# Second layer of a four-layer recurrent kernel: logits beside B and C, state product on column groups, next tile's first steps inside the last expert

## The reference

```python
# mixer: Mamba-2 (SSD), 8 heads of 64, state 16
zxbcdt = u @ W_in.T                       # z 512, x 512, B 16, C 16, dt 8
dt  = softplus(zxbcdt[..., -8:] + dt_bias)
xBC = silu(causal_conv4(xBC))
y   = ssd(x * dt, A * dt, B, C) + x * D   # chunked scan
y   = rmsnorm(y * silu(z)) * norm_w
s   = y @ W_out.T
# ffn: 8 experts, all computed, gated by a 1.5-entmax found by 25 bisection steps
logits = xt @ Wr + br
gates  = entmax_bisect(logits, n_iter=25)
h = relu(xt @ W1[e] + b1[e]);  y = h @ W2[e] + b2[e];  out = sum_e y * gates[:, e]
```

## Time and profile before

| | |
|---|---|
| median of 3 runs | 4324.44 us (4317.86 to 4325.86) |
| the profiled execution, its own time | 4321.67 us |
| its span in the trace | 4319.8 us |
| mean granted TensorE clock | 0.987 |
| PE busy | 4179.0 us, 97% |
| DVE busy | 2288.0 us, 53% |
| ACT busy | 1636.5 us, 38% |
| layer 1 in the trace | about 634 to 2765 us |

### The profile page before, as it was taken

The page is one execution under the profiler, slowest core; times in us unless marked ns, Lnnn a source line. Parts: engine busy times, 40 slices in busy tenths (PEclk is TensorE's granted clock), DMA queues, the critical chain, the costliest instruction groups (busy, mean ns, idle before and its releaser), DMA issues. The chain is left out here.

```text
span 4319.8 us, 55665 instructions
## 1 busy us (share of the span) xinstructions
PE 4179.0 (97%) x19509; PEld 2441.8 (57%) x19509; DVE 2288.0 (53%) x5759; ACT 1636.5 (38%) x3125; POOL 305.9 (7%) x412
## 2 busy tenths in 40 slices
PE   6999989999999999999999999999998998999999
PEld 3545455666756666666666766656666554333333
DVE  6666655252342523315243252287787887666765
ACT  3444443223232232323223232354544321455555
POOL 0122211101010020100201001000000000000000
PEclk9999999999999999999999999999999999999999
DMA  3111111112112121211212112100000000111110
GB/s 88 17 17 26 26 46 60 70 59 99 69 65 84 59 81 69 78 71 61 82 64 85 66 68 89 55 1 1 1 1 8 14 1 22 19 21 23 26 24 22
DMA packets 52690, 198.17 MB, mean 46 GB/s; under 512 B 10257, under 2 KB 20145, under 8 KB 35385
## 3 DMA queue, kind: packets, MB, share of 16 engines
q1 hardware_dynamic: 51616, 194.57, 13.7%
q10 hardware_dynamic: 816, 0.20, 0.0%
HBM read 171.14 MB, written 4.46 MB: 41 GB/s over the span
## 5 line engine op out<-in xcount | busy, mean ns | idle before, releaser
L1135 PE MATMUL l_exp_out<-l_w,l_hidden 128*128 128x256 f32 x4096 | 905.4, 381 | 0.3
L1125 PE MATMUL l_hid<-l_xn_t,l_w 128*128 128x512 f32 x2048 | 893.0, 594 | 1.0 <-ACT l_hidden L1259 1.0
L1135 PEld LDWEIGHTS l_exp_out<-l_w,l_hidden 128*128 128x128 f32 x4096 | 774.1, 190 | 114.2 <-issue 4.3
L1259 ACT ACTIVATE l_hidden<-l_hid,l_w 128x512 f32<-128x512 f32 x512 | 351.4, 686 | 933.4 <-PE l_hid L1125 933.4
L1125 PEld LDWEIGHTS l_hid<-l_xn_t,l_w 128*128 128x128 f32 x2048 | 387.8, 190 | 472.5 <-issue 454.3
L507 DVE TENSOR_REDUCE l3f_row_max<-l3f_bank 128x1 f32<-128x512 f32 x512 | 327.6, 685 | 177.3 <-PE l3f_bank L387 176.9
L1451 DVE SCALAR_TENSOR_TENSOR l_moe<-l_exp_out,l_gates,l_moe 128x256 f32<-128x256 f32 x256 | 123.7, 483 | 463.5 <-PE l_exp_out L1135 457.0
L463 ACT ACTIVATE l3f_prob_t<-l3f_bank 128x512 f32<-128x512 f32 x512 | 277.2, 596 | 206.4 <-PE l3f_bank L394 206.3
L504 DVE CUSTOM_DVE_ANT_0 l_masked<-l_bank,l_mask 128x256 f32<-128x256 f32 (+3 forms) x512 | 226.7, 486 | 156.9 <-PE l_bank L387 156.0
L394 PE MATMUL l3f_bank<-l3f_qk_t 32*128 32x512 f32 x1024 | 303.0, 637 | 0.9 <-ACT l3f_prob_t L463 0.5
L387 PE MATMUL l3f_bank<-l3f_qk_t 32*128 32x512 f32 x1024 | 297.2, 643 | 5.3 <-DMA l3f_qk_t<-l3f_packed 5.1
(11 more groups left out here) (480 smaller groups left out, 5600.0 us busy)
## 6 DMA issues: line engine op xcount, KB each, us to landing
l_w<-in_w SPq DMA_DIRECT2D x128, 1024.0 KB, 5.0
l_mix<-l_cum SPq DMA_DIRECT2D x32, 512.0 KB, 4.0
l_qk_t<-l_packed SPq DMA_DIRECT2D x128, 64.0 KB
l3f_qk_t<-l3f_packed SPq DMA_DIRECT2D x128, 64.0 KB
all_x<-in_x SPq DMA_DIRECT2D x8, 512.0 KB, 6.7
out_x<-all_x SPq DMA_DIRECT2D x7, 512.0 KB, 3.0
l_hidden<-in_fp4w SPq DMA_DIRECT2D x1, 2304.0 KB
l_qk_t<-l_max_rows SPq DMA_DIRECT2D x128, 2.0 KB
```

The source lines that it names most:

```text
L1125: ins = nc.tensor.matmul(bank[:, :], w1[:, e % 2, c, f * P:(f + 1) * P], xn_t[:, c, :], start=c == 0, stop=c == CT - 1)
L1135: ins = nc.tensor.matmul(bank[:, 0:C], hidden[:, e % 2, f, j * P:(j + 1) * P], w2[:, e % 2, f, :], start=f == 0, stop=f == HF - 1)
L1259: hid.empty(nc.scalar.activation(hidden[:, e % 2, f, :], bank[:, :], ACT.Relu, bias=w[:, B1][:, e * HF + f:e * HF + f + 1]), (e, f))
```

## The change

- **Logits beside B and C.** The weights of B and C (64 columns with padding) and of dt and the logits (16) are copied side by side into `wbcs` by DVE at the layer's start. One product `bc` of 80 output rows and 512 columns replaces `xb4`; ACT copies its last 16 rows to `small_t` (the storage of `c_scaled`) and its first 48 to `xbc`. `small_in` becomes four transposes of 16 x 128.
- **Order.** `bc` belongs to the next tile's first steps. For all but the last tile, `ss` stands ahead of `expert_in(7)`, and that is cut in three: features 0 to 2, `normal_in`, features 3 to 5, `small_rows_in` (`bc`), features 6 and 7. `xn_t` gets a second slot. `small_in` keeps its place within `expert_out(6)`.
- **State on column groups.** `st{j}` is four products of 128 columns, each to its own 32 output partitions; DVE copies or adds four pieces instead of one.
- **Inner projection copied first.** ACT copies the next tile's `xb0` to `xb3` before it takes the silu of `moe`, not after. ACT's stream is unrolled.
- **Bisection.** Two turns behind each `expert_sum(7, j)` instead of one (14 in the tile, was 10), 11 after it (was 15), and these stand before the last products of the tile on DVE, not behind them.

```diff
-        first_names = [f"xt{c}" for c in range(CT)] + ["small"]
-        names = [f"xb{f}" for f in range(XF)] + ...
+        first_names = [f"xt{c}" for c in range(CT)] + ["bc", "small"]
+        names = [f"xb{f}" for f in range(FT)] + ...
+            def small_rows_in(ring, it, t):
+                ring.wait_emptied_through(pe, it, [f"xt{c}" for c in range(CT)])
+                bank = ring.open(pe, it, "bc")
+                for c in range(CT):
+                    ins = nc.tensor.matmul(bank[0:S_ROW + SH + E, :], wbcs[:, c, :], xn_t[:, t % 2, c, :], start=c == 0, stop=c == CT - 1)
+                ring.fill(ins, "bc")
+
             def small_in(ring, it):
...
-                    for c in range(CT):
-                        ins = nc.tensor.matmul(bank[:, j * (SH + E):(j + 1) * (SH + E)], xn_t[:, c, j * P:(j + 1) * P], ws[:, c, :],
-                                               start=c == 0, stop=c == CT - 1)
+                    ins = nc.tensor.transpose(bank[:, j * (SH + E):(j + 1) * (SH + E)], small_t[:, j * P:(j + 1) * P],
+                                              ident[0:SH + E, 0:SH + E])
...
+            pe.wait_ge(small_weights, 1)
             normal_in(first, 0, 0)
+            small_rows_in(first, 0, 0)
             small_in(first, 0)
...
-                        jobs.fill(nc.tensor.matmul(bank[0:SN, :], b_tok[:, j, :], x_dec[:, j % 2, :], start=True, stop=True), f"st{j}")
+                        for g in range(TJ):
+                            ins = nc.tensor.matmul(bank[g * SLOT:g * SLOT + SN, 0:P], b_tok[:, j, :], x_dec[:, j % 2, g * P:(g + 1) * P],
+                                                   start=True, stop=True)
+                        jobs.fill(ins, f"st{j}")
...
+                        if e == 6:
+                            pe.wait_ge(squares_summed, (b + 1) * TJ + 1)
...
+                        if e == 6 and not is_last:
+                            expert_in(7, range(0, 3))
+                            normal_in(jobs, b, b + 1)
+                            expert_in(7, range(3, 6))
+                            small_rows_in(jobs, b, b + 1)
+                            expert_in(7, range(6, HF))
+                        elif e + 1 < E:
                             expert_in(e + 1)
...
+            def small_rows_in(ring, it):
+                bank = ring.wait_filled(act, it, "bc")
+                nc.scalar.activation(small_t, bank[S_ROW:S_ROW + SH + E, :], ACT.Copy)
+                ring.empty(nc.scalar.activation(xbc[0:C_ROW + SN, FT, TAPS - 1:T + TAPS - 1], bank[0:C_ROW + SN, :], ACT.Copy), "bc")
+            normal_in(first, 0, 0)
+            small_rows_in(first, 0)
             nc.scalar.activation(neg_a[:, :], w[:, ALOG], ACT.Exp).then_inc(act_prepared, 1)
...
                 else:
+                    inner_in(b + 1)
                     exp_out.wait_emptied_through(act, b, [(E - 1, j) for j in range(TJ)])
                     nc.scalar.activation(moe[:, :, :], moe[:, :, :], ACT.Silu).then_inc(gate_ready, 1)
...
+            V.tensor_copy(wbcs[:, :, 0:S_ROW], wbc)
+            V.tensor_copy(wbcs[:, :, S_ROW:], ws).then_inc(small_weights, 1)
...
-                                ins = V.tensor_tensor(state[:, :], state[:, :], bank[0:SN, :], ALU.add)
+                                for old, new in groups:
+                                    ins = V.tensor_tensor(old, old, new, ALU.add)
...
-                                route(st, 1)
+                                route(st, 1 if e == 6 else 2)
...
+                    route(st, BISECT - 14)
+                    route_end(st)
                     jobs.wait_emptied_through(dve, b, [f"o{j}" for j in range(TJ)])
                     dve.wait_ge(gate_ready, b + 1)
                     st.link(V.tensor_tensor(s[:, :, :], s[:, :, :], moe[:, :, :], ALU.mult))
                     V.tensor_tensor(x_all[:, b], x_all[:, b], s[:, :, :], ALU.add)
-                    route(st, BISECT - 10)
-                    route_end(st)
```

More of the change, by code:

```diff
@@ L1124, in expert_in, with expert_out @@
                         for c in range(CT):
-                            ins = nc.tensor.matmul(bank[:, :], w1[:, e % 2, c, f * P:(f + 1) * P], xn_t[:, c, :],
+                            ins = nc.tensor.matmul(bank[:, :], w1[:, e % 2, c, f * P:(f + 1) * P], xn_t[:, b % 2, c, :],
                                                    start=c == 0, stop=c == CT - 1)
                         hid.fill(ins, (e, f))
-                def expert_out(e, between=None):
+                def expert_out(e, between=()):
                     pe.wait_ge(w2_loaded[e % 2], 16 * (b * (E // 2) + e // 2 + 1))
@@ L1137, in expert_out @@
                         exp_out.fill(ins, (e, j))
-                        if j == 0 and between is not None:
-                            between()
+                        if j < len(between):
+                            between[j](jobs, b)
                 def chunk_scores(j):
@@ L1164, in chunk_products @@
                         bank = jobs.open(pe, b, f"st{j}")
-                        jobs.fill(nc.tensor.matmul(bank[0:SN, :], b_tok[:, j, :], x_dec[:, j % 2, :], start=True, stop=True), f"st{j}")
-                for f in range(XF):
-                    bank, m = jobs.open(pe, b, f"xb{f}"), rows_of(f)
+                        for g in range(TJ):
+                            ins = nc.tensor.matmul(bank[g * SLOT:g * SLOT + SN, 0:P], b_tok[:, j, :], x_dec[:, j % 2, g * P:(g + 1) * P],
+                                                   start=True, stop=True)
+                        jobs.fill(ins, f"st{j}")
+                for f in range(FT):
+                    bank = jobs.open(pe, b, f"xb{f}")
                     for c in range(CT):
-                        lhs = wx[:, c, f * P:(f + 1) * P] if f < FT else wbc[:, c, 0:m]
-                        ins = nc.tensor.matmul(bank[0:m, :], lhs, xn_t[:, c, :], start=c == 0, stop=c == CT - 1)
+                        ins = nc.tensor.matmul(bank[:, :], wx[:, c, f * P:(f + 1) * P], xn_t[:, b % 2, c, :], start=c == 0, stop=c == CT - 1)
                     jobs.fill(ins, f"xb{f}")
@@ L1175, in sequence @@
                     for c in range(CT):
-                        ins = nc.tensor.matmul(bank[:, :], wz[:, c, f * P:(f + 1) * P], xn_t[:, c, :], start=c == 0, stop=c == CT - 1)
+                        ins = nc.tensor.matmul(bank[:, :], wz[:, c, f * P:(f + 1) * P], xn_t[:, b % 2, c, :], start=c == 0, stop=c == CT - 1)
                     jobs.fill(ins, f"z{f}")
@@ L1192, in sequence @@
                     if e >= 1:
-                        if e + 1 < E:
+                        if e == 6:
+                            pe.wait_ge(squares_summed, (b + 1) * TJ + 1)
+                            bank = jobs.open(pe, b, "ss")
+                            for j in range(TJ):
+                                ins = nc.tensor.matmul(bank[:, j * SN:(j + 1) * SN], sum_sq[:, j, :], ones[:, 0:SN], start=True, stop=True)
+                            jobs.fill(ins, "ss")
+                        if e == 6 and not is_last:
[5 more added lines that the diff above has]
+                        elif e + 1 < E:
                             expert_in(e + 1)
@@ L1218, in sequence @@
                             chunk_scores(e - 1)
[L1219 to L1226, removed]
                         if e == 7:
@@ L1235, in sequence @@
                                 jobs.fill(ins, f"o{j}")
-                    expert_out(e, (lambda: small_in(jobs, b)) if e == 6 and not is_last else None)
+                    expert_out(e, (small_in,) if e == 6 and not is_last else ())
             for b in range(B):
@@ L1243, in _, with normal_in, inner_in @@
             act.wait_ge(ahead.w_loaded, 16)
-            def normal_in(ring, it):
+            def normal_in(ring, it, t):
                 for c in range(CT):
                     bank = ring.wait_filled(act, it, f"xt{c}")
-                    ring.empty(nc.scalar.activation(xn_t[:, c, :], bank[:, :], ACT.Copy), f"xt{c}")
-            normal_in(first, 0)
+                    ring.empty(nc.scalar.activation(xn_t[:, t % 2, c, :], bank[:, :], ACT.Copy), f"xt{c}")
+            def small_rows_in(ring, it):
+                bank = ring.wait_filled(act, it, "bc")
+                nc.scalar.activation(small_t, bank[S_ROW:S_ROW + SH + E, :], ACT.Copy)
+                ring.empty(nc.scalar.activation(xbc[0:C_ROW + SN, FT, TAPS - 1:T + TAPS - 1], bank[0:C_ROW + SN, :], ACT.Copy), "bc")
+            def inner_in(b):
+                jobs = last_ring if b == B - 1 else ring
+                for f in range(FT):
+                    bank = jobs.wait_filled(act, b, f"xb{f}")
+                    jobs.empty(nc.scalar.activation(xbc[:, f, TAPS - 1:T + TAPS - 1], bank[:, :], ACT.Copy), f"xb{f}")
+            normal_in(first, 0, 0)
+            small_rows_in(first, 0)
             nc.scalar.activation(neg_a[:, :], w[:, ALOG], ACT.Exp).then_inc(act_prepared, 1)
@@ L1285, in sequence @@
```

(23 more changed lines are left out.)

14 lines of the change are left out of this document (7 added, 7 removed).

## The result

The changed kernel takes 4303.55 us (median of 5 runs, 4301.23 to 4305.90), the kernel before 4317.87 us (median of 5, 4314.29 to 4325.86; three of the five are the runs of the table ahead, whose median was 4324.44). The ratio is 0.9957, 95% interval 0.9945 to 0.9969: between 13 and 24 us less. It is not the plain quotient of the two medians, which is 0.9967, or 14.3 us. It is faster beyond the 0.2% that the prediction named, and 4303.55 lies in its range.

A forecast was written before the change was run, and what follows sets the result against it. PE, busy 97% of the span, was taken as the bound, except at the layer's start, set by the chain ending in DVE's bisection. -14.6 - 10.1 + 4.9 + 4.0 = -15.8 us gave a 4308.6 us median; range 4301 to 4321.

The forecast's parts named there:

- the 0.2% that the prediction named: Whole kernel: what a measurement can tell from no change, 8.6 us; below 4315.8 is faster, above 4333.1 slower.
- the four terms of the sum: State products -14.6 us, logits -10.1, DVE in expert 7 +4.9, the layer's start +4.0.
- from the saving to the median: Whole kernel: span 4305.9 us by the saving, plus 2.8 for the median of 4324.44, so 4308.6, 0.37% less.
- State on column groups: State products on PE: 0.35 us instead of 0.96 each, 24 times, 14.6 us saved, bounds 0 and 14.6.
- The 0.24 us: State product by the skill page's speedup of up to 4x: the term would be 17 us instead of 14.6.
- Logits beside B and C: `small_in` as four transposes: 0.27 us instead of 1.71, 1.44 saved in each of seven tiles, 10.1 us.
- Expert 7's input in pieces: Steps inserted in `expert_in(7)`: no more PE work, cost nothing, or up to 0.2 us per tile.
- ACT at the boundary: ACT's copies, table loads and silus at the next tile's start just fit: cost 0, up to 0.3 us per tile.
- The rival that ACT would be late: Tile boundary, or DVE later in expert 7: 1.5 us per tile, +10.5, 4319 us; chance 0.17.
- DVE in expert 7: Second bisection turn frees banks late; PE loses 0.7 us per tile (0.3 to 1.0), +4.9 us in seven tiles.
- The layer's start: Longer chain before the first bisection: `route_start` from 639.98 to about 644.0, +4.0 us, bounds 2.4 and 5.
- The saving: Whole kernel: the terms sum to -15.8 us.

The follow-up runs named there:

- the old start: The changed kernel with the first tile's dt columns and logits by the 16 old products and the Exp ahead of ACT's copies: 4303.07 us, ratio 0.9951.
- the silu first: The changed kernel with ACT's silu of the expert sums ahead of its copies of the inner projection: 4316.18 us, ratio 0.9981 to the kernel before.

## Why the prediction's mechanism held, and which step failed

The costs, the waits and the path came out as reckoned, and none of the four terms of the sum was off by 1 us. The step that failed is the last one of the sum, from the saving to the median in us; it stands at the end of this section.

**State on column groups: right.** Predicted 0.35 us per product and 14.6 us in all; measured 0.34 and, as the only change, 14.6. The weights of 16 columns overlap here as well as those of 32 in the earlier trace rows. The 0.24 us that the prediction gave beside it as an estimate was not reached: 0.34 is 2.8 times faster than 0.96. DVE's four pieces take 1.17 us, the one piece before took 0.67, and DVE's next wait for PE is still 1.79 (DVE's timeline in the kernel before, which goes ahead of the earlier trace rows, and in the changed one):

```profile
1289.26 0.67 DVE L1508 COPY l_state<-l_bank 16x512 f32<-16x512 f32 x1
```
```profile
1292.34 1.17 DVE L1543 COPY l_state<-l_bank 16x128 f32<-16x128 f32 x4
1295.30 0.48 DVE L1484 SCALAR_TENSOR_TENSOR l_moe<-l_exp_out,l_gates,l_moe 128x256 f32<-128x256 f32 x1 [1.79 <-PE l_exp_out L1146]
```

That a faster TensorE may move the limit to the evacuation of PSUM (the Trainium skill, TensorEngine Tiling (Array Packing), Performance Considerations) did not come true in this trace: DVE's room shrank from 2.91 us to 1.79, by 0.50 for its own extra work and by 0.62 because PE's next product comes that much earlier. Behind an addition, where DVE also scales the state, 1.19 us are left of 2.30.

**Logits beside B and C: right in kind, a little less.** The transposes take 0.35 us within an expert instead of the 0.27 that the row behind other transposes had: 1.36 us saved per tile instead of 1.44, 9.5 us instead of 10.1.

**Expert 7's input in pieces: right, at nothing lost.** The steady tile adds up: 1.86 (three products, 0.62 each) and 1.36 saved, 0.81 lost in expert 7 make 2.41; measured 2.54. The prediction took the product for B and C to cost the same in its new place. It costs a little less (PE's timeline in the kernel before and in the changed one):

```profile
1456.00 7.13 PE L1176 MATMUL l_bank<-l_xn_t,l_w 128*128 128x512 f32 x16
```
```profile
1408.40 1.88 PE L1111 MATMUL l_bank<-l_xn_t,l_wbcs 128*80 128x512 f32 x4
1410.12 3.60 PE L1136 MATMUL l_hid<-l_xn_t,l_w 128*128 128x512 f32 x8
...
1456.62 7.03 PE L1189 MATMUL l_bank<-l_xn_t,l_w 128*128 128x512 f32 x16
```

The inner projection's x with `xb4` took 8.81 us (1447.19 to 1456.00), without it 6.87 (1449.75 to 1456.62): `xb4` cost 1.94 us, `bc` costs 1.72. The 0.22 and smaller differences of both signs make the 0.13 that the terms leave. What the cost of nothing rests on was shown by joining the pieces: 1.1 us per tile.

**ACT at the boundary: right, with nearly no room.** In the changed kernel ACT does what was reckoned, with four table loads from 1457.44 on, of which the first is shown:

```profile
1457.44 1.28 ACT L1356 ACT_TABLE_LOAD   x1
...
1464.18 2.07 ACT L1301 ACTIVATE l_z_act<-l_bank 128x512 f32<-128x512 f32 x4
1466.11 0.71 ACT L1288 ACTIVATE l_hidden<-l_hid,l_w 128x512 f32<-128x512 f32 x1
1467.12 0.69 ACT L1288 ACTIVATE l_hidden<-l_hid,l_w 128x512 f32<-128x512 f32 x1 [0.30 <-PE l_hid L1136]
```

With S = 1449.75, the start of the next tile's inner projection, relu 0 ends at S + 17.1 (reckoned S + 17.3), and the second relu already waits for PE again. `expert_in(0)` starts at 1463.49, S + 13.7 (reckoned S + 14.0); with two features of 1.7 its third starts at S + 17.2 by this estimate, so 0.1 us was left, as reckoned. PE has no wait for ACT in a steady tile. The rival that ACT would be late did not come.

**DVE in expert 7: right.** Predicted 0.7 us per tile with PEld waiting 0.4 and 0.8; the weight loads of the changed kernel:

```profile
1441.94 3.32 PEld L1146 LDWEIGHTS l_exp_out<-l_w,l_hidden 128*128 128x128 f32 x16 [0.45 <-DVE l_moe L1484]
1446.19 3.32 PEld L1146 LDWEIGHTS l_exp_out<-l_w,l_hidden 128*128 128x128 f32 x16 [0.94 <-DVE l_moe L1484]
```

0.45 and 0.94, and PE loses 0.81 us: 5.7 us in all, where 4.9 was the term. The gates are ready at 1481.5 and asked for at 1489.3: 7.8 us to spare, where 7 were reckoned.

**The layer's start: right.** Predicted + 4.0, measured + 4.2, by the reckoned chain (timelines of ACT and DVE in the changed kernel). While `bc` runs, 641.86 to 645.50, the granted clock is 0.51, which is the lower level of 1.2 GHz, as the prediction took it to be:

```profile
645.57 0.59 ACT L1269 ACTIVATE l_c_scaled<-l_bank 16x512 f32<-16x512 f32 x1 [3.81 <-PE l_bank L1111]
646.17 0.59 ACT L1270 ACTIVATE l_xbc<-l_bank 48x512 f32<-48x512 f32 x1
646.67 0.20 ACT L1280 ACTIVATE l_neg_a<-l_w 128x8 f32<-128x8 f32 x1
```
```profile
646.89 0.17 DVE L1411 TENSOR_SCALAR l_neg_a<-l_neg_a 128x8 f32<-128x8 f32 x1 [6.74 <-ACT l_neg_a L1280]
...
648.43 0.21 DVE L1421 TENSOR_TENSOR l_small<-l_bank,l_w 128x64 f32<-128x64 f32 x1
```

DVE waits 6.74 us for an Exp that needs nothing from what stands before it, and only then does the preparation that the bisection is queued behind. But the Exp is the smaller part of the loss (PE's timeline in the changed kernel):

```profile
646.82 0.42 PE L1118 MATMUL l_bank<-all_cst,l_c_scaled 16*128 16x16 f32 x4 [1.28 <-ACT l_xbc L1270]
```

The transposes end at 647.24, so with the Exp moved alone the bisection could start at best some 1.2 us earlier than 648.43. By this estimate the other 3 us are the later start of PE, `bc` at the lower clock and ACT's two copies. That all of it lies on the path is shown: the first gates come 4.1 us later, and 3.9 us earlier in the old start.

**The saving: right.** Predicted - 15.8 us; the layer is 15.8 us shorter in the traces. The terms as read from the rows are - 14.9 (24 times 0.62), - 9.5, + 5.7 and + 4.2, together - 14.5. The rest is 0.13 us in each of six steady tiles, 0.3 more in the first tile, and 0.2 that is not placed. That it comes out to the tenth is luck: errors of 0.6, 0.8 and 0.2 one way and of 1.6 the other cancel.

**The step that failed: from the saving to the median.** It reads "The median shown is 4324.44, 2.8 above; so 4308.6 for the median". It took the median of three runs for a fixed level to subtract from. Two more runs of the same kernel brought that median to 4317.87, which is 6.6 us lower, almost half of what the change saves. So the 4308.6 stand only 9.3 us, 0.22%, below the kernel that the changed one was measured against, where the change measured 0.43% (0.31 to 0.55), twice that. From 4317.87 the same saving gives 4302.1, and 4303.55 was measured. The forecast in us was 5 too high; the forecast as a share, 0.37%, lies in the interval.

Which of the medians is the odd one stays open. Over 23 later runs the kernel before had a median of 4324.3 again, near the one that was used. From there the changed kernel's five runs lie 20.8 us lower, 5 more than the layer accounts for, and there is no long series of the changed kernel. What is shown is that a median of three or five is uncertain here by some 6 us.

## What to carry to other kernels

A product with few output rows can be cut along its moving columns and spread over column groups: the same instructions took 0.98 us in one group and 0.34 in four. In a kernel where one engine is busy all the time, look for the few places where another chain sets the time (here the start of the layer, and the banks that DVE frees in expert 7): what is moved into such a chain counts in full, and must be kept out of it even if it is free everywhere else. Work that is spread to shorten a tail can lengthen the step that it is put into; ask first whether the tail was waited for at all. And forecast a saving of a few tenths of a per cent as a share, or for the stretch that the change touches: a level in us inherits the scatter of the few runs that it is taken from.

## What the runs showed of the hardware

The time at which layer 1 starts differs from trace to trace by up to 6 us (633.5 to 639.7), in code that no version changed. It goes with the TensorE clock that was granted in the first 80 us of the run. The windows of 20 to 80 us, in the kernel before and in the changed one:

```profile
20.00:80.00 60.00, 49.74 (x236) 22.38 (x235) 35.53 (x143) 15.63 (x33) 4.41 (x10) 0.89 0.29 73
```
```profile
20.00:80.00 60.00, 50.07 (x216) 22.68 (x215) 32.59 (x131) 14.28 (x30) 4.43 (x10) 0.80 0.29 73
```

Both are means of stretches at 1.2 and at 2.4 GHz. At 0.80 instead of 0.89 PE gets 20 instructions less done in the same 60 us. Of the ten traces, the five with 0.89 there start layer 1 at 633.5 to 634.5, the five with 0.80 at 636.8 to 639.7. What decides which of the two an execution gets was not found. Behind layer 1, too, unchanged code takes from 1551.4 us (the changed kernel) to 1560.6 (the silu first), 1556.0 in the kernel before. In the two profiled executions of this change the 4.3 us that layer 1 starts later and the 4.6 us that the rest takes less nearly cancel, by chance, so that the spans differ by 16.1 and the layer by 15.8. It is why differences of a few microseconds were read from the layer and not from the whole.
